# Score and maximum tiles of two heads in pairs of PSUM banks, with one ACTIVATE or TENSOR_REDUCE per pair, and one fixed bank for the gate network

## The reference

```python
xn = layernorm(x)                                   # x: 4 x 2048 x 256, fp32
qkv = xn @ w_qkv + b_qkv; q, k, v = split, 16 heads of 16
scores = einsum('bhid,bhjd->bhij', q, k) / 4
scores = where(j >= i, scores, -inf)                # each query sees itself and later keys
s = (softmax(scores) @ v) @ w_out + b_out
h = s0 * ([xn, -xn] @ W0); h = relu(h) * 2          # W0, W1, W2 hold +1 and -1
h = s1 * (h @ W1);         h = relu(h) * 2
g = silu(s2 * (h @ W2))
out = x + s * g
```

## Time and profile before

| | |
|---|---|
| runs of the kernel | 2552.58 us, median of 3 (2552.55 to 2552.8) |
| the profiled execution | 2555.14 us; its span from first to last instruction 2553.4 us |
| busy share of the span | PE 96%, DVE 71%, ACT 60%, POOL 36% |
| mean granted TensorE clock | 0.983 of full speed |
| instructions on the tile of exponentials | 2560 ACTIVATE (L1141), 1216.9 us busy |
| reads for the maxima | 1536 TENSOR_REDUCE (L1196), 976.9 us busy; 1024 masked ones (L1193) |

### The profile page before, as it was taken

One profiled execution on the slowest core, in us unless ns is written; L12 is line 12 of the kernel. 1 busy time (PEld: TensorE's weight loads), 2 busy tenths in 40 slices (PEclk: granted clock), 3 DMA queues, 4 the chain that ended last, 5 costly groups with the idle time before them and its releaser, 6 DMA issues.

```text
span 2553.4 us, 50994 instructions
## 1 busy us (share of the span) xinstructions
PE 2455.9 (96%) x17616; PEld 1478.7 (58%) x17616; DVE 1823.4 (71%) x4516; ACT 1542.0 (60%) x3135; POOL 913.5 (36%) x1080
## 2 busy tenths in 40 slices
PE   7989999999999999999999999999999999999986
PEld 6877555555555555555555555555555555555552
DVE  7767867677777777777777777777767777777712
ACT  5652656666666666666666665666666665666642
POOL 1014223332433434243433433343434434343532
PEclk9998999999999999999999999999999999999986
DMA  8981111011111212131212212121212122121321
GB/s 317 356 328 45 39 29 53 21 53 29 52 35 40 74 47 69 41 86 34 77 43 69 58 35 79 44 78 41 78 36 81 42 55 67 43 73 42 95 88 47
DMA packets 157805, 192.67 MB, mean 75 GB/s; under 512 B 65276, under 2 KB 102076, under 8 KB 157560
## 3 DMA queue, kind: packets, MB, share of 16 engines
q1 hardware_dynamic: 156600, 189.41, 24.4%
q10 hardware_dynamic: 960, 0.00, 0.0%
HBM read 112.13 MB, written 76.14 MB: 74 GB/s over the span
## 4 chain that ended last, share of the span: by engine, by line
PE 86%; DMA 4%; DVE 3%; ACT 2%; POOL 2%; issue 2%; SPq 1%; POOLq 0%; ACTq 0%; DVEq 0%
PE b_ps L1083 21%; PE b_pv_ps L1061 21%; PE b_ps L1029 18%; PE b_ps L1041 11%; PE b_ps L1080 5%; PE b_ps L1087 5%; PE b_ps L1106 3%; DMA a_xs<-L_attn_x 2%; ACT b_probs L1141 1%; PE a_qk_ps L290 1%; DMA b_xs<-L_attn_x 1%; DVE a_stats L396 1%; DVE a_qk_parts L434 1%; DVE b_part_max L1196 1%; PE b_ps L1049 1%
## 5 line engine op out<-in xcount | busy, mean ns | idle before, releaser
L1141 ACT ACTIVATE b_probs<-b_ps 128x512 f32<-128x512 f32 (+3 forms) x2560 | 1216.9, 534 | 687.2 <-PE b_ps L1029 684.8
L1196 DVE TENSOR_REDUCE b_part_max<-b_ps 128x1 f32<-128x512 f32 x1536 | 976.9, 682 | 296.3 <-PE b_ps L1041 295.0
L1193 DVE CUSTOM_DVE_ANT_0 b_ps<-b_ps,k_mask 128x512 f32<-128x512 f32 (+3 forms) x1024 | 483.2, 515 | 255.0 <-PE b_ps L1041 251.6
L1061 PE MATMUL b_pv_ps<-b_probs,k_vst 128*32 128x512 f32 (+3 forms) x5120 | 604.6, 544 | 12.7 <-issue 8.6
L1029 PE MATMUL b_ps<-k_qst,k_kst 50*128 50x512 f32 (+3 forms) x2560 | 594.2, 461 | 6.2 <-DMA k_qst<-b_max_parts 3.2
L1029 PEld LDWEIGHTS b_ps<-k_qst,k_kst 50*128 50x128 f32 x2560 | 239.9, 184 | 548.7 <-DVE b_part_max L1196 193.0
L1083 PE MATMUL b_ps<-b_u_hi,k_w 128*128 128x256 f32 x2048 | 534.3, 296 | 3.9 <-POOL b_u_lo L965 3.8
L1041 PE MATMUL b_ps<-k_kst,k_qst 48*128 48x512 f32 (+3 forms) x2560 | 493.4, 379 | 28.3 <-ACT b_probs L1141 20.7
L1083 PE MATMUL b_ps<-b_u_lo,k_w 128*128 128x256 f32 x2048 | 519.9, 289 | 0.0
L1083 PEld LDWEIGHTS b_ps<-b_u_hi,k_w 128*128 128x128 f32 x2048 | 392.6, 192 | 62.9 <-issue 47.4
L963 POOL CAST b_u_hi<-b_u 128x512 fp32r<-128x512 f32 x256 | 156.1, 610 | 753.4 <-ACT b_u L1169 753.2
(11 more groups left out here) (101 smaller groups left out, 1849.9 us busy)
## 6 DMA issues: line engine op xcount, KB each, us to landing
qk_parts<-a_qk_parts SPq DMA_DIRECT2D x64, 512.0 KB, 3.8
k_kst<-qk_parts SPq DMA_DIRECT2D x384, 64.0 KB, 2.3
k_qst<-qk_parts SPq DMA_DIRECT2D x384, 64.0 KB, 2.3
a_xs<-L_attn_x SPq DMA_DIRECT2D x16, 512.0 KB, 5.6
xn_T<-a_xT SPq DMA_DIRECT2D x16, 512.0 KB, 5.1
v_plain<-a_v_out SPq DMA_DIRECT2D x16, 512.0 KB, 5.0
k_xf<-xn_T SPq DMA_DIRECT2D x32, 256.0 KB, 3.3
b_v_in<-v_plain SPq DMA_DIRECT2D x64, 128.0 KB, 2.6
```

Source lines behind the costliest of these rows:

```text
L1061: mm = pe.matmul(pv_ps[h * VW:(h + 1) * VW, 0:cols], vst[:, kb // TT, kb % TT, h, :], probs[:, s % P_SLOTS, h, 0:cols], start=start, stop= ...
L1141: act.activation(probs[:, s % P_SLOTS, h, 0:cols], ps[:, banks[place, half][0], 0:cols], ACT.Exp, scale=HD ** -0.5).then_inc(exp_done, 1)
L1193: dve.tensor_tensor_reduce(src, src, mask[:, 0:CHUNK - k0 % CHUNK], 1.0, -3.0e38, ALU.add, ALU.max, dst).then_inc(ring_read, 1)
L1196: dve.tensor_reduce(dst, src, AX_X, ALU.max).then_inc(ring_read, 1)
```

## The change

The scores of two heads, and the two score tiles of an M, now lie in two neighbouring banks, and `ps` is three such pairs: `[P, 3, 2, 512]`. Every S, M, negmax, project and the like takes the next pair in turn, whole, though the small ones use one bank of it; the pair's user before, three claims back, must have been read in full. The network has the seventh bank, `f_ps`, for all its uses: a use waits until ACT has read the one before.

ACT exponentiates a pair with one ACTIVATE of 2 x up to 512 columns, and DVE reduces a pair with one TENSOR_REDUCE that gives two maxima. The masked reads stay two, and the second signals. Only the second matmul of a pair raises its semaphore, so all counts of `s_ready`, `exp_done`, `ring_ready` and `ring_read` count pairs. The order of events, the matmuls and their sizes are as they were.

```diff
-BANKS = 7
+BANK_PAIRS = 3
...
-    free = list(range(BANKS))
-    counts = {"exp": 0, "ring": 0, "f": 0}
-    for at, (what, *arg) in enumerate(order):
...
-        for k in range(number):
-            use = ("F", arg[0]) if what == "F" else (at, k)
-            if use not in out:
-                bank = free.pop(0)
-                counts[kind] += 1
-                out[use] = (bank, *last.get(bank, (None, 0)))
-                last[bank] = (kind, counts[kind])
-            if what != "F" or arg[8]:
-                free.append(out[use][0])
+    counts = {"exp": 0, "ring": 0}
+    for at, (what, *_) in enumerate(order):
+        kind = {"S": "exp", "M": "ring", "negmax": "ring", "fold_bias": "ring", "project": "ring", "last_sums": "ring",
+                "last_project": "ring"}.get(what)
+        if kind:
+            pair = len(out) % BANK_PAIRS
+            counts[kind] += 1
+            out[at] = (pair, *last.get(pair, (None, 0)))
+            last[pair] = (kind, counts[kind])
     return out
...
-        ps = pb("ps", [P, BANKS, CHUNK])
+        ps = pb("ps", [P, BANK_PAIRS, HALVES, CHUNK])
+        f_ps = pb("f_ps", [P, FPU, PIECE])
...
-                    outs = [claimed((place, half)) for half in range(HALVES)]
+                    dst = claimed(place)
                     for half in range(HALVES):
...
-                        pe.matmul(outs[half][:, 0:cols], keys, qst[rows, c, pair, 0:cols],
-                                  start=True, stop=True).then_inc(s_ready, 1)
+                        mm = pe.matmul(dst[:, half, 0:cols], keys, qst[rows, c, pair, 0:cols], start=True, stop=True)
+                    mm.then_inc(s_ready, 1)
...
                     if lo == 0:
-                        claimed(("F", use))
+                        if use > 0:
+
+                            pe.wait_ge(f_read, use)
...
-                    for half in range(HALVES):
-                        h = pair * HALVES + half
...
-                        act.wait_ge(s_ready, g * SCORES + s * GH + h + 1)
-                        act.activation(probs[:, s % P_SLOTS, h, 0:cols], ps[:, banks[place, half][0], 0:cols], ACT.Exp,
-                                       scale=HD ** -0.5).then_inc(exp_done, 1)
+                    heads = slice(pair * HALVES, (pair + 1) * HALVES)
...
+                    act.wait_ge(s_ready, g * SCORES + s * PAIRS + pair + 1)
+                    act.activation(probs[:, s % P_SLOTS, heads, 0:cols], ps[:, banks[place][0], :, 0:cols], ACT.Exp,
+                                   scale=HD ** -0.5).then_inc(exp_done, 1)
...
+                        for j in range(HALVES):
+                            at = row + j * PAIRS * TT
+                            op = dve.tensor_tensor_reduce(src[:, j, 0:cols], src[:, j, 0:cols], mask[:, 0:cols], 1.0, -3.0e38,
+                                                          ALU.add, ALU.max, part_max[ib // TT % 2][:, at, kc:kc + 1])
+                        op.then_inc(ring_read, 1)
+                    else:
+                        dve.tensor_reduce(part_max[ib // TT % 2][:, row::PAIRS * TT, kc], src[:, :, 0:cols], AX_X, ALU.max
+                                          ).then_inc(ring_read, 1)
```

More of the change, by code:

```diff
@@ L1007, in claimed @@
             def claimed(use):
-                bank, reader, count = banks[use]
+                pair, reader, count = banks[use]
                 if reader == "exp":
@@ L1013, in claimed @@
                     pe.wait_ge(ring_read, count)
-                elif reader == "f":
-                    pe.wait_ge(f_read, count)
-                return ps[:, bank]
+                return ps[:, pair]
             for place, (what, *arg) in enumerate(order):
@@ L1037, in _ @@
                         pe.wait_ge(k_loaded[kc], (g + 1) * HALVES * PARTS * DMA)
-                    outs = [claimed((place, j))[:, 0:CHUNK - k1] for j in range(HALVES)]
+                    dst = claimed(place)
                     for j in range(HALVES):
                         rows = slice(j * HALF, j * HALF + DEPTH)
-                        pe.matmul(outs[j], qst[rows, c, pair, i * P:(i + 1) * P],
-                                  kst[rows, k_slot(kc, g % 2), pair, k1:CHUNK], start=True, stop=True
-                                  ).then_inc(ring_ready, 1)
+                        mm = pe.matmul(dst[:, j, 0:CHUNK - k1], qst[rows, c, pair, i * P:(i + 1) * P],
+                                       kst[rows, k_slot(kc, g % 2), pair, k1:CHUNK], start=True, stop=True)
+                    mm.then_inc(ring_ready, 1)
                 elif what == "negmax":
                     g, c = arg
-                    dst = claimed((place, 0))
+                    dst = claimed(place)[:, 0]
                     pe.wait_ge(padded, 1)
@@ L1072, in _ @@
                             pe.wait_ge(u_split, need)
-                    dst = f_bank(use)
+                    dst = f_ps
                     depth = KH if kind == "L0" else KF
@@ L1168, in _ @@
                         layer = 0 if kind == "L0" else 1
-                        act.activation(u[:, split % U_SLOTS], f_bank(use), ACT.Relu,
+                        act.activation(u[:, split % U_SLOTS], f_ps[:], ACT.Relu,
                                        scale=kept.sign[:, layer:layer + 1]).then_inc(f_read, 1)
@@ L1187, in _ @@
                     pair, ib, kc, k0 = units[at]
-                    for j in range(HALVES):
-                        row = (j * PAIRS + pair) * TT + ib % TT
-                        dst, src = part_max[ib // TT % 2][:, row, kc:kc + 1], filled((place, j))[:, 0:CHUNK - k0 % CHUNK]
-                        if kc == ib // TT:
-                            dve.tensor_tensor_reduce(src, src, mask[:, 0:CHUNK - k0 % CHUNK], 1.0, -3.0e38, ALU.add,
-                                                     ALU.max, dst).then_inc(ring_read, 1)
-                        else:
-                            dve.tensor_reduce(dst, src, AX_X, ALU.max).then_inc(ring_read, 1)
+                    cols = CHUNK - k0 % CHUNK
+                    src, row = filled(place), pair * TT + ib % TT
+                    if kc == ib // TT:
+                        for j in range(HALVES):
[6 more added lines that the diff above has]
+                                          ).then_inc(ring_read, 1)
                 elif what == "neg":
@@ L1241, in _ @@
                 elif what == "last_sums":
-                    src = ps[:, banks[place, 0][0]]
+                    src = ps[:, banks[place][0], 0]
                     for half in range(2):
@@ L1252, in _ @@
                     rows = slice(half * FPU, (half + 1) * FPU)
-                    src = ps[:, banks[place, 0][0]].rearrange("p (t h) -> p t h", h=H)
+                    src = ps[:, banks[place][0], 0].rearrange("p (t h) -> p t h", h=H)
                     dve.wait_ge(last_projected, half + 1)
```

43 lines of the change are left out of this document (18 added, 25 removed).

## The result

| | us | ratio to the kernel before, 95% interval |
|---|---|---|
| before | 2552.69, median of 4 | |
| after | 2598.69, median of 4 (2597.37 to 2603.0) | 1.0168 [1.0147, 1.0189] |
| after, again, beside another group of runs | 2600.48, median of 4 | 1.0179 [1.0155, 1.0203] |

The change makes the kernel 46 us slower by the medians, and 43 to 46 by the ratios 1.0168 and 1.0179 (the first is not the quotient of the two medians beside it, which is 1.0180). The forecast was 2597. The profiled execution took 2603.0 us, its span 2601.3; against the profile of before that is 47.9 us more of span.

The account below looks back on a forecast made before the run. PE was taken as the bound (96% busy). M 35, negmax 10, other S 7 and lead 8 made 60 us, less 15 for double counting: 45 us, forecast 2597 us, range of 8 in 10 2553 to 2620.

Parts of the forecast that it names:

- the 15 taken off: Deduction of 15 us from the 60 us sum, for waits of PE counted twice within the same step.
- M, 35 us: M's load must wait for both heads' exponentials, mostly behind network ends: 35 us slower in sum.
- The one ACTIVATE: One exponential over a pair's 1024 columns takes 1.026 us, 0.06 less than two in a row.
- the 80 to 150 among the signs: Sign to look for in the profile: ACT's busy time down by 80 to 150 us.
- old stalls: M's existing waits where no use has ended: 0.06 shorter in some 90 places, 5 us saved, 2 lost elsewhere.
- negmax, 10 us: negmax takes a whole pair that DVE is still reading, in 30 of its 64 places: 0.34 us each.
- Other S, 7 us: The turn brings some 20 S to a pair still being read: 0.33 us each.
- The lead, 8 us: In the lead, network uses wait for the single bank: 0.53 us each, up to 1.2 behind layer 2, 12 places.
- Fewer signals: Rival: matmul signals cost PE time and 2560 of them go; some 2571 us, chance 0.06.
- Waits taken up elsewhere: Rival: old stalls shrink by more than 0.06 each, new waits stay in the free 0.11; 2540 to 2560, chance 0.14.
- Heavier: Rival: two-bank reads save nothing, late M delays the next relu, no double counting; 2623 us, chance 0.12.
- forecast case: Main case of the prediction: a time of 2565 to 2615 us, chance 0.68.

Follow-up runs that it names:

- e4: Kernel before with one edit: the network has a fixed bank and the other six go round singly; 2615.22 us, ratio 1.0238.
- g2: Changed kernel with ACT's read of a finished network use moved behind the exponential of pair 1; 2587.57 us, ratio 1.0130.
- e2: Changed kernel with two ACTIVATEs a pair again, claims and signals still by pairs; 2621.01 us, ratio 1.0255.
- n1: Changed kernel with negmax 0.15 of a step later, behind the network span; 2598.06 us, ratio 1.0171.
- e3: Changed kernel with two ACTIVATEs and two TENSOR_REDUCEs a pair again, claims and signals still by pairs; 2625.49 us, ratio 1.0275.
- e1: Changed kernel in which the first matmul of each S and M pair signals too, 2560 signals more; 2605.25 us, ratio 1.0200.
- f2: Changed kernel with a second bank for the network in the lead, where M goes round two pairs; 2594.79 us, ratio 1.0153.

## Why the prediction was right

- **The sum.** 45 us forecast, 43 to 46 measured in the runs, 47.9 in span. The mechanism held. That the sum came within 3 us is in part luck: the miss at other S was made up by the 15 taken off, and that of the lead by the clock (both below).
- **M, 35 us.** 34.3 by the distances in the two timelines, and it stands where it was said to: 39.9 at the network ends against 38, of which 9.8 behind layer 2 against 11, and -2.6 where no use had ended against -3. The prices of its kinds came out within 0.02 us at the places shown (0.04 at the negmax). e4 and g2 confirm the mechanism, but its name should be another: not that M needs "both halves", which it needed before where no use had ended, but that the rotation lost a bank.
- **The one ACTIVATE.** 1.024 us and 0.06 saved were right. ACT is 76 us less busy, which fits the 79 of the working and just misses the 80 to 150 among the signs. What the read is worth to PE was never summed: -3 us were booked for old stalls and the rest lay hidden in the prices of the kinds; undone, it costs 20 us (e2), where I then expected 12. Without it the change would stand at +66.
- **negmax, 10 us.** 9.2 in the distances; but n1 shows that most of it can't be had by moving negmax, as S then waits.
- **Other S, 7 us.** Not found: the distances from M, the network and PV to the next S together changed by -6.7 us. This is the term that was mis-sized. Why S lost nothing wasn't tried. The reductions, 0.06 shorter, are at most a small part (2.6 us): e3 has the single ones and the same distances are still 4.1 below those of before. That the stalls of PE in the same step give DVE time is left, and isn't shown. The 15 us taken off for double counting covered this: 35 + 10 + 8 alone are 53, and 34.3 + 9.2 + 8.7 were measured as 52.2, with -5.4 beside them where I had +7 and -15. No row stood behind the 15; that it was near what was needed is luck.
- **The lead, 8 us.** 8.7. But it isn't all waiting: the granted clock was 0.80 from 160 to 230 us against 0.90 before, and a network matmul that took 0.28 us at full clock shows 0.41 to 0.42 at 184 us. At equal clock the waits cost 5.1 (e4), and the single bank's loss is 4.9 to 8.7 over e1, e4 and the two profiles of the change. So the term was some 3 too large for its mechanism, and what came with the lower clock, which wasn't in the sum, filled the gap.
- **The rivals.** Fewer signals: excluded by e1. Waits taken up elsewhere: M's waits on ACT grew from 43 to 68 us, so it fell. Heavier: its 2623 lies above the interval, whose upper end, 1.0189, is 2601.
- **A slip in the range.** The lead's waits and half of M's are 8 + 17.5 = 25.5 us, not the 32 by which the lower end of the forecast case was set, so 2571 and not 2565. Two thirds of the 15 and the 11 of the 0.06 are 21, so 2618 at the upper end and not 2615. Neither touches the forecast.

## What to carry to other kernels

With a shared pool of PSUM banks, count how many claims lie between a tile and the next use of its bank, and compare the readers' time with PE's over that distance; a bank that is set aside for one user shortens the distance for all the others, here by one in seven at +61 us. A merged read saves its fixed part only where somebody waits for that reader, and a late block is not cured by placing it later without looking at who takes over its bank. An event's own load time, the end of the reader in the trace and the delay between them (0.11 us here) priced M's changed claims within 0.02 us a place; the S claims, priced from another block's row, came out wrong in sign.

## What the runs showed of the hardware

- One ACTIVATE over two PSUM banks runs at the pace of one bank: 598 ns for 512 columns, 1024 for 1024.
- A semaphore signal on a matmul with other matmuls behind it costs 2 to 3 ns by the middles of the ratios (e1), at most 7 by the ends of their intervals, and perhaps nothing.
- One TENSOR_REDUCE over two banks saves its fixed part too: 682 ns for 512 columns, 1223 for 1024.
- A weight load that waits for a reader of ACT starts 0.11 to 0.12 us after that reader's end (1443.81 to 1443.92, 1234.96 to 1235.08).
- The clock of the lead differs between profiles of kernels with the same matmuls: 0.80 granted from 160 to 230 us in the change, 0.85 in its second profile, 0.88 in e1 and 0.90 in e4, all with the network's single bank; 0.90 in the kernel before and 0.95 in f2, which lack its waits. With e4 at 0.90, that the waits lower the clock isn't shown; the lead of the change, at 0.80, took 3.6 us more than that of e4, at 0.90.
